# A GNN edge kernel: the count codes' one-hots in rows of eight columns, and one compare as tensor_tensor

## The reference, cut to what matters

```python
edge_weight = (deg[src] * deg[dst]) ** -0.5
edge_msg = relu(edge_attr @ W1e + b1e) @ W2e + b2e
agg = segment_sum((h[src] + edge_msg) * edge_weight, dst)
combined = (1 + gin_eps) * h + agg
out = relu(combined @ W1n + b1n) @ W2n + b2n + h
y = x + out * rsqrt(mean(out * out) + RMS_EPS) * rms_w
```

## Time and profile before

| what | before |
|---|---|
| device time, median of 3 runs | 1160.48 us (1159.67 to 1161.26) |
| span of the profiled execution | 1158.9 us |
| PE, PEld busy | 1061.3 us, 764.4 us |
| DVE busy | 964.8 us |
| ACT busy | 734.5 us |
| POOL busy | 809.0 us |
| TensorE granted clock, mean | 0.993 |

### The profile page before, as it was taken

How to read it: one execution, slowest core, us unless ns; L and a number is a source line. 1 busy time by engine, 2 the same in 40 slices (tenths; PEclk the granted TensorE clock), 3 DMA queues, 4 the chain that set the end, 5 groups by cost and what they waited for, 6 DMA issues and landing times. The chain is left out here.

```text
span 1158.9 us, 35277 instructions
## 1 busy us (share of the span) xinstructions
PE 1061.3 (92%) x12293; PEld 764.4 (66%) x12293; DVE 964.8 (83%) x4508; ACT 734.5 (63%) x1317; POOL 809.0 (70%) x826
## 2 busy tenths in 40 slices
PE   0335999999999999999999999999999999999986
PEld 0322677777677777777777777777777777777753
DVE  7799988888888888888888888878888888888468
ACT  6953766666666666666666666666666666666535
POOL 1046777777777777777777777777777777777464
PEclk9999999999999999999999999999999999999988
DMA  6035444444444444444444444444444444443463
GB/s 221 1 142 156 133 118 120 129 118 120 130 119 118 129 120 118 129 120 119 128 120 119 128 119 119 130 118 120 128 118 120 129 118 120 130 119 80 129 255 119
DMA packets 67388, 145.56 MB, mean 126 GB/s; under 512 B 24163, under 2 KB 25750, under 8 KB 66832
## 3 DMA queue, kind: packets, MB, share of 16 engines
q1 hardware_dynamic: 41120, 88.27, 24.5%
q0 software_dynamic: 25088, 51.83, 18.8%
q10 hardware_dynamic: 1008, 3.21, 0.8%
HBM read 136.67 MB, written 6.57 MB: 124 GB/s over the span
## 5 line engine op out<-in xcount | busy, mean ns | idle before, releaser
L1008 POOL DMA_INDIRECT arena<-node_rows,idx x784 | 765.9, 977 | 247.7 <-issue 199.5
L1168 ACT ACTIVATE arena<-bank 128x686 f16<-128x686 f32 x414 | 375.9, 908 | 204.9 <-PE bank L1078 204.0
L1160 ACT ACTIVATE arena<-bank 128x512 f32<-128x512 f32 (+1 forms) x460 | 250.6, 555 | 157.3 <-PE bank L1033 141.0
L1089 PE MATMUL bank<-t_words,arena 128*126 128x256 f16 x2254 | 302.8, 275 | 0.4 <-ACT arena L1168 0.4
L1234 DVE SCALAR_TENSOR_TENSOR arena<-iota_h,hi_f,bank 128x98 f32<-128x98 f32 x828 | 226.1, 309 | 82.3 <-PE bank L1043 82.1
L1033 PE MATMUL bank<-w1e,arena 64*128 64x128 f32 x3312 | 253.9, 273 | 0.0
L1218 DVE TENSOR_SCALAR arena<-iota_c,code 128x343 f16<-128x343 f16 x828 | 241.6, 334 | 6.6 <-PE bank L1078 4.8
L1089 PEld LDWEIGHTS bank<-t_words,arena 128*126 128x126 f16 x2254 | 238.0, 136 | 1.7 <-ACT arena L1168 0.7
L1033 PEld LDWEIGHTS bank<-w1e,arena 64*128 64x128 f32 x3312 | 222.4, 191 | 0.0
L1078 PE MATMUL bank<-arena 128*128 128x343 f16 x828 | 190.6, 312 | 0.2
L1204 DVE TENSOR_SCALAR arena<-arena,part_f 128x256 f16<-128x256 uint8 x414 | 147.1, 355 | 0.8 <-DVE t_words L612 0.6
(11 more groups left out here) (199 smaller groups left out, 863.7 us busy)
## 6 DMA issues: line engine op xcount, KB each, us to landing
arena<-in_attr SPq DMA_DIRECT2D x138, 384.0 KB
arena<-low_src SPq DMA_DIRECT2D x48, 288.0 KB, 5.4
arena<-node_rows,idx POOLq DMA_INDIRECT x784
node_rows<-arena SPq DMA_DIRECT2D x1, 3160.5 KB, 8.9
arena<-in_x ACTq DMA_DIRECT2D x7, 448.0 KB, 10.9
arena<-in_x SPq DMA_DIRECT2D x6, 512.0 KB, 13.4
out<-arena SPq DMA_DIRECT2D x12, 224.0 KB
arena<-node_rows SPq DMA_DIRECT2D x4, 516.0 KB, 8.8
```

The lines of the kernel that those rows point to most:

```text
L1008: nc.gpsimd.indirect_dma_start(out=edge_rows[:, u, j, 0:ROW], out_offset=None, in_=table, in_offset=bass.IndirectOffsetOnAxis(ap=idx[:, u, ...
L1089: mm = nc.tensor.matmul(x_sum[0:XC, 0:2 * D], strip[:, u, k, :], T16[:, k, :], start=k == 0, stop=k == NBLK - 1)
L1160: ins = nc.scalar.activation(out.rearrange("p (j o) d -> p o j d", o=2), of, ACT.Relu)
L1168: nc.scalar.activation(strip[:, u, :, 2 * p * W:2 * p * W + 2 * W].rearrange("p k (t w) -> p t k w", t=2), pair_bank[:, :].rearrange("p (t ...
```

## The change

Three things. `code_oh` gets rows of eight columns for each of the 49 high parts, of which the first seven are written and read: a tile's one-hot is now 49 pieces of 7 at a pitch of 8, in 392 columns instead of 344. DVE's compare (L1218) writes in that form, and PE's count matmul (L1078) reads its moving operand in that form; it still has 343 columns, in the same order. And `turn_low` (L1204) compares by `tensor_tensor`, with the partition's number read again for each of the 256 elements, where it was a `tensor_scalar` with a per-partition scalar.

```diff
@@ -45,6 +45,7 @@
 W = 7
 GW = 32
 CW = NBLK * W
+WS = W + 1
@@ -214,7 +215,7 @@
-        loop.code_oh = take(2 * 2 * (CW + 1) // 2).bitcast(F16).rearrange("p (u t c) -> p u t c", u=2, t=2)
+        loop.code_oh = take(2 * 2 * NBLK * WS // 2).bitcast(F16).rearrange("p (u t k w) -> p u t k w", u=2, t=2, w=WS)
@@ -1075,7 +1076,7 @@
                 for j in range(2):
-                    mm = nc.tensor.matmul(pair_bank[:, j * 512:j * 512 + CW], low_oh[:, (u + 2 * p // LB) % 2, :, 2 * p % LB + j], code_oh[:, (u + p) % 2, j, 0:CW],
+                    mm = nc.tensor.matmul(pair_bank[:, j * 512:j * 512 + CW], low_oh[:, (u + 2 * p // LB) % 2, :, 2 * p % LB + j], code_oh[:, (u + p) % 2, j, :, 0:W],
                                           start=True, stop=True)
@@ -1201,8 +1202,8 @@
-                nc.vector.tensor_scalar(low_t[:, k % RL, :, :].rearrange("p t e -> p (t e)"), low_b[:, u, 2 * k * 128:(2 * k + 2) * 128],
-                                        part_f[:, 0:1], None, ALU.is_equal).then_inc(low_t_ready, 1)
+                nc.vector.tensor_tensor(low_t[:, k % RL, :, :].rearrange("p t e -> p (t e)"), low_b[:, u, 2 * k * 128:(2 * k + 2) * 128],
+                                        part_f[:, 0:1].broadcast_to((128, 256)), ALU.is_equal).then_inc(low_t_ready, 1)
@@ -1215,7 +1216,7 @@
                 for j in range(2):
-                    ins = nc.vector.tensor_scalar(code_oh[:, (u + p) % 2, j, 0:CW], iota_c[:, :], code[:, column(c), 2 * p + j:2 * p + j + 1],
+                    ins = nc.vector.tensor_scalar(code_oh[:, (u + p) % 2, j, :, 0:W], iota_c[:, :].rearrange("p (k w) -> p k w", w=W), code[:, column(c), 2 * p + j:2 * p + j + 1],
                                                   None, ALU.is_equal)
```

## The result

The changed kernel takes 1187.95 us (median of 4 runs, 1187.82 to 1188.13) where the kernel before takes 1160.30 on the same chip (4 runs, 1159.67 to 1161.26): a ratio of 1.0238, 95% interval 1.0223 to 1.0252. It is 2.4% slower; 1.3% was forecast (1176 us, range 1164 to 1190). The profiled execution's span went from 1158.9 to 1186.1 us, 27.2 more where 15.4 was reckoned. Every line from the count matmul on has a number one higher than before: L1079 is the count matmul, L1205 the low parts' compare, L1219 the codes' compare, L1287 `keep_x`'s reduce, L1090 the spread matmuls.

A forecast was written before the change was run, and what follows sets the result against it. PE's instruction stream was taken as the bound, DVE mattering only where PE waits. 13.5 us at slot 1 plus 1.9 at the start on the profiled 1158.9 gave 1174.3; runs' median 1.6 above: 1176 us, range 1164 to 1190.

The forecast's parts named there:

- The bound and the tie: PE's own stream sets the period; slot 1's first L1089, waiting for DVE's `keep_x`, has no slack, mean excess now 0.02 us.
- L1204, +75 ns: Low parts' compare on DVE: as tensor_tensor over 256 elements it takes 413 ns instead of 338 at least.
- L1218, +90 ns: Codes' compare on DVE: writing 49 pieces halves its speed, 383 ns instead of 293; ends nothing and +262.
- The chain, +0.33 us a step: DVE's path from `pick_s(8)` to slot 1: two L1204 and two L1218 add 330 ns; 13.5 us over 43 steps.
- the slowest rival: L1218 falls to one element at a time, DVE needs 23.8 us a step and sets the period: about 1265 us, chance 0.06.
- The start, 1.9 us: Step 0's six short slots, set by DVE, lose 1.5 us, and the priming's five or so `turn_low` 0.4.
- PE's read, "I take nothing": L1078's moving operand hops after every seven columns; hops overlap the columns and cost nothing, at most 1.4 ns each, 59 us.
- a rival at 0.3 ns a hop: PE reads the pieces slowly: 15 ns a matmul, 12 us over 828, giving 1185 us; chance 0.10.
- Its own sign of being wrong: The period moving in all slots at once, which would be PE's read; only slot 1 was to grow, the period to 21.98.
- Freed port: Rival: DVE no longer holds what POOL needs, compares and gathers shorten, and the kernel is faster, 1158.5 us; chance 0.04.
- near 945: Expected profile sign: POOL's gathers at about 945 ns, where they averaged 977 before.

## Why the prediction was right, and what it missed

**The bound and the tie: right.** PE's stream sets the period, and slot 1 is the only slot of steps 2 to 44 in which DVE's delay reaches it. One part of the change at a time, each with its own delay at slot 1, and the exchange in `keep_x`, which takes 10.8 us back, show it.

**L1204, +75 ns: right.** 414 ns at the median, 413 reckoned; its hold on DVE grew by 0.07 us.

**L1218, +90 ns: right where it counts, short in the duration.** The row says 402 ns at least and 422 at the median, 19 and 39 over the 383. But the path feels the time from one start to the next: 0.305 us after, 0.22 before, so +85 ns. The prediction left open how the source is encoded. The trace's record of L1219's operands has it: the source is one run of 343, though the program writes it as rows, and the destination 49 rows of 7. The Trainium skill (Vector Engine (DVE) Microarchitecture Reference, 5.1 Performance modes) has the second port dropped when odd outermost counts of source and destination differ; the halving and the vanished maxima agree with it.

**The chain, +0.33 us a step: 0.31 measured.** PE's longer slots 8 and 0 then gave 0.08 of it back, so slot 1 got 0.23 and the loop 9.9 us where 13.5 were forecast (43 x 0.31 is 13.3; likewise 2.1 x 44 in the slowest rival is 92, not 94). Without the hops, in 7 rows of 49, slot 1 got 0.28.

**The start, 1.9 us: 2.0 measured**, though the forecast had DVE alone in it. Slot 1 of step 2 begins 1.95 us later in the kernel after, 1.80 in the one with 7 rows of 49 and 0.26 in the one where PE's read alone is changed, so DVE has most of it.

**PE's read, "I take nothing": wrong.** This is the step that failed. It measures 20 ns a matmul, 828 x 20 ns = 16.6 us, more than all of DVE's share. The prediction had it as a rival at 0.3 ns a hop and 1185 us, with a chance of 0.10; the hop costs 0.42. Its own sign of being wrong came, too: the period moved in all slots at once, by 0.04 us each, where all slots but one were to stay. With that term the prediction's own sum is 1174.3 + 16.6 - 3.4 = 1187.5, against a span of 1186.1. The bound was well placed, nothing to 1.4 ns. The choice inside it was not: L379 showed 91 ns for 49 hopping columns, weight load included, so it left room for a cost and gave no reason for none. That the pieces follow each other almost without a gap was the only reason given, and it is no price. And a stream that has no slack anywhere is where a small price is paid 828 times in full. That the measured 1188 us still lie in the range of 1164 to 1190 is owed to the range's width and not to the sum: more than half of the 27.6 us come from a term that was put at nothing.

**Freed port: right not to count on it.** That the compares and the gathers got in each other's way is in the trace of the kernel before: all 131 L1218 and all 24 L1204 that took over 60 ns more than their median have the end of a gather inside them, and of the others about one in four has. In the kernel after no compare is that long. But the gathers did not get shorter: their mean went from 977 to 994 ns, and was 996 with the low compare alone changed. The forecast of "near 945" holds for the median (947) alone, and that stood at 945 before. The Trainium skill (SBUF — State Buffer, Who interferes with whom) says that a DVE instruction with two SBUF inputs contends with a GpSimd instruction that reads SBUF. Rows agree in so far as the mean is higher in each kernel with the low compare as tensor_tensor than before; it is 982 with that compare left and the codes' alone changed, so the low compare isn't the only cause. From 100 us on, no gather of the kernel before takes over 1.4 us, 24 do with the low compare alone changed, and two in the kernel after. What a gather reads from SBUF, and when, no run here shows.

## What to carry to other kernels

When the bounding engine has no slack, a change in how it reads an operand is the first term to price, and "the pieces nearly touch" is no price: look for its cost per instruction times their number before that of the helper engine. A tie between two engines costs next to nothing until one is slowed, and then what it is slowed by beyond the other; here an exchange of two instructions, so that what PE waits for comes first, was worth 10.8 us in the slow kernel and about 1.8 in the fast one. Price an instruction on a chain by the time to the next start, not by its own duration.

## What the runs showed of the hardware

- The count matmul pays for reading its moving operand in pieces: 343 f16 columns take 309 to 312 ns in one run or in 7 pieces, 329 to 331 in 49 pieces at a pitch of 8 or 9, and 336 at a pitch of 16. Between the starts of two of them lie 146 ns in one run, 150 in 7 pieces, 166 in 49 at a pitch of 8 or 9, and 177 at 16. That is 0.42 ns for each of 48 hops at a pitch of 8, about one column's time at the granted clock of 1.00 (2.4 GHz). All pieces tried had an odd length.
- The codes' compare in 49 rows of 7 has a duration of 402 and 422 ns (minimum and median) and in 7 rows of 49 one of 376 and 388, while the next start comes 0.305 and 0.300 us later. Why the duration differs by 26 to 34 ns and the spacing by 5 stays open.
- In the kernel before, each of the 131 longest codes' compares and the 24 longest low compares (over 60 ns above the median) has the end of a gather inside it. In their changed forms both have lost these cases (maxima 536 to 443 and 522 to 452 ns), and the gathers are no shorter. What holds these was not found.
